# Linear attention without a projection of the values: exponentials of k times the normalised input, then the value weights on the 128x128 result

## What is computed

```
xn = _rmsnorm(x, g1)                                  # over the channels of a token
qkv = jnp.einsum('oc,bchw->bohw', w_qkv, xn)
q, k, v = (qkv[:, 0], qkv[:, 1], qkv[:, 2])
k = jnp.concatenate([mk, k], axis=-1)                 # memory tokens in front
v = jnp.concatenate([mv, v], axis=-1)
q = jax.nn.softmax(q, axis=-2) * attn_scale
k = jax.nn.softmax(k, axis=-1)                        # over the tokens
context = jnp.einsum('bhdn,bhen->bhde', k, v)
out = jnp.einsum('bhde,bhdn->bhen', context, q)
out = jnp.einsum('oc,bchw->bohw', w_out, out) + b_out[None, :, None, None]
return _rmsnorm(out, g2)                               # added to the block's input
```

## Time and profile before

| | us |
|---|---|
| runs | 493.48, 493.88, 495.92 |
| median | 493.88 |
| span of the profiled execution | 491.7 |
| PE busy | 442.3 (90%) |
| DVE busy | 384.4 (78%) |
| ACT busy | 275.3 (56%) |
| POOL busy | 222.1 (45%) |

### The profile page before, as it was taken

One profiled execution on the slowest core, in us unless ns is written; L12 is line 12 of the kernel. 1 busy time (PEld: TensorE's weight loads), 2 busy tenths in 40 slices (PEclk: granted clock), 3 DMA queues, 4 the chain that ended last, 5 costly groups with the idle time before them and its releaser, 6 DMA issues. The chain is left out here.

```text
span 491.7 us, 8244 instructions
## 1 busy us (share of the span) xinstructions
PE 442.3 (90%) x2398; PEld 372.7 (76%) x2398; DVE 384.4 (78%) x754; ACT 275.3 (56%) x828; POOL 222.1 (45%) x187
## 2 busy tenths in 40 slices
PE   2659675999999999999999999999999999998796
PEld 1538464888888888887888888888888888876675
DVE  4461578989798979897988979898989798987531
ACT  2346567574738475657567574848575657552110
POOL 5404345544545372736454455546372736333120
PEclk9977968899999999999999999999999999999799
DMA  7202020203021120303030302012030202021011
GB/s 214 118 0 87 1 87 1 85 3 128 1 86 45 39 91 1 128 0 128 0 128 0 128 0 92 36 47 81 13 117 1 87 0 88 0 87 43 2 43 43
DMA packets 9563, 27.99 MB, mean 57 GB/s; under 512 B 1969, under 2 KB 3009, under 8 KB 9537
## 3 DMA queue, kind: packets, MB, share of 16 engines
q1 hardware_dynamic: 9536, 27.68, 16.0%
HBM read 19.29 MB, written 8.39 MB: 56 GB/s over the span
## 5 line engine op out<-in xcount | busy, mean ns | idle before, releaser
L1126 PE MATMUL ps_conv<-pad_hi,w_lo 128*128 128x512 f32 (+1 forms) x288 | 121.8, 423 | 0.0
L1126 PE MATMUL ps_conv<-pad_hi,w_hi 128*128 128x512 f32 (+1 forms) x288 | 118.7, 412 | 2.9 <-POOL w_lo L496 2.9
L1126 PE MATMUL ps_conv<-pad_lo,w_hi 128*128 128x512 f32 (+1 forms) x288 | 119.4, 414 | 0.0
L549 ACT ACTIVATE qkv<-ps_qkv,scale 128x384 f32<-128x384 f32 x128 | 70.3, 582 | 32.1 <-PE ps_qkv L1046 30.2
L496 POOL TENSOR_TENSOR w_lo<-w_full,w_hi 128x1152 fp32r<-128x1152 f32 x16 | 42.5, 2659 | 92.1 <-ACT w_hi L607 53.7
L464 POOL TENSOR_TENSOR q_exp<-q_exp,q_rsum 128x1024 f32<-128x1024 f32 x16 | 30.6, 1913 | 89.2 <-DVE q_rsum L778 89.2
L1126 PEld LDWEIGHTS ps_conv<-pad_hi,w_lo 128*128 128x128 f32 x288 | 55.6, 193 | 13.5
L1126 PEld LDWEIGHTS ps_conv<-pad_hi,w_hi 128*128 128x128 f32 x288 | 55.7, 193 | 13.0 <-POOL w_lo L496 3.7
L1126 PEld LDWEIGHTS ps_conv<-pad_lo,w_hi 128*128 128x128 f32 x288 | 55.6, 193 | 9.4
L561 ACT ACTIVATE q_exp<-q_exp 128x1024 f32<-128x1024 f32 x16 | 17.0, 1061 | 68.1 <-DVE q_exp L764 68.1
L1044 PE MATMUL ps_qkv<-wqkv_hi,x_hi 128*128 128x384 f32 x128 | 46.1, 360 | 5.2 <-ACT qkv L549 4.7
(11 more groups left out here) (122 smaller groups left out, 980.4 us busy)
## 6 DMA issues: line engine op xcount, KB each, us to landing
xa<-in_x_dram SPq DMA_DIRECT2D x16, 512.0 KB, 4.2
xb<-in_x_dram SPq DMA_DIRECT2D x16, 512.0 KB, 4.9
out_dram<-result SPq DMA_DIRECT2D x16, 512.0 KB, 2.9
expert_raw<-_conv_expert_weight_dram SPq DMA_DIRECT2D x1, 1728.0 KB, 8.8
fc<-in_L_conv_fc_w_dram SPq DMA_DIRECT2D x1, 384.0 KB, 4.3
wqkv_raw<-in_L_conv_w_qkv_dram SPq DMA_DIRECT2D x1, 192.0 KB, 3.4
wout_raw<-in_L_conv_w_out_dram SPq DMA_DIRECT2D x1, 64.0 KB, 2.5
bias_raw<-in_L_conv_b_out_dram SPq DMA_DIRECT2D x1, 64.0 KB, 2.4
```

What stands on the lines that cost most here:

```text
L549: nc.scalar.activation(qkv[:, t, 0:QKV], ps_qkv[t % 2][:, 0:QKV], ACT.Copy, scale=scale1[:, t:t + 1]).then_inc(qkv_done, 1)
L1126: last = mm(into, weight[:, tap, :], pixels[:, top + down:bottom + down, columns_in], start=(n == 0), stop=(n == 3 * TAPS - 1))
```

## The change

The projection computes q and k only (`wqk_hi`, `wqk_lo`; 256 columns instead of 384). The v part is replaced by associativity. While the transposed x is still in `ps_qkv`, ACT copies it to `x_nt` (`x_copy`, twice 128x512, behind each `squares1`), and POOL multiplies it by `scale1` (`x_scale`, 128x1024, behind `filters_low`). `key_contexts` on PE multiplies the exponentials of k by `x_nt`. Its result is divided later: `k_sums` takes the reciprocal of the sums, `k_x_evacuate` (ACT) copies the result out, `key_context_transpose` (PE) transposes it, `x_k_evacuate` (ACT) copies that, and the new `contexts` (PE) multiplies it by the value weights and adds the memory tokens' part. `context_mask` (DVE) keeps the heads' blocks, `mixes` and `mix_evacuate` follow as before, the latter with the reciprocal.

Orders change too. On PE `mixes` moves behind both halves of `x_transpose` and behind `group_variances`; then come two products of the convolution, `routing`, and only then `outputs`. Before it was `mixes`, `x_transpose`, `group_variances`, `outputs`, `routing`. The core of the diff:

```diff
+            def x_scale(b, p):
+                pool.wait_ge(x_nt_done, 2 * (b + 1))
+                pool.wait_ge(scale1_done, b + 1)
+                nc.gpsimd.tensor_tensor(x_nt[:, :, 0:C], x_nt[:, :, 0:C],
+                                        scale1[:, :].unsqueeze(2).to_broadcast((128, NT, C)),
+                                        ALU.mult).then_inc(x_scaled_done, 1)
...
                 do(filters_low, t, p, 4)
+                do(x_scale, t, p, 2)
                 do(q_normalise, t, p, 2)
...
+            def x_copy(b, p, h):
+                if past(b, 1):
+                    act.wait_ge(k_x_ps, b)
+                act.wait_ge(ssq1_sum_done, 2 * b + h + 1)
+                nc.scalar.activation(x_nt[:, NT // 2 * h:NT // 2 * (h + 1), 0:C],
+                                     ps_qkv[h][:, :].rearrange("p (t c) -> p t c", c=C), ACT.Copy).then_inc(x_nt_done, 1)
...
-                nc.scalar.activation(qkv[:, t, 0:QKV], ps_qkv[t % 2][:, 0:QKV], ACT.Copy, scale=scale1[:, t:t + 1]).then_inc(qkv_done, 1)
+                nc.scalar.activation(qk[:, t, :], ps_qkv[t % 2][:, 0:QK], ACT.Copy, scale=scale1[:, t:t + 1]).then_inc(qkv_done, 1)
...
+                do(k_x_evacuate, t, p, 2)
                 do(q_evacuate, t, p, 2, 0)
-                do(context_evacuate, t, p, 2)
+                do(x_k_evacuate, t, p, 2)
                 do(q_evacuate, t, p, 2, 1)
                 do(image_high, t, p, 3)
                 do(squares1, t, p, 1, 0)
+                do(x_copy, t, p, 1, 0)
                 do(squares1, t, p, 1, 1)
+                do(x_copy, t, p, 1, 1)
...
+                do(context_mask, t, p, 2)
                 do(gn2_centre, t, p, 3)
                 do(mix_evacuate, t, p, 2)
                 turn(variances, t, p, 0)
...
-                do(context_sums, t, p, 1)
+                do(k_sums, t, p, 1)
                 do(gn2_aggregate, t, p, 2)
-                do(context_scale, t, p, 1)
...
-                mm(o, x1_hi[:, tile(t)], wqkv_hi[:, :], start=True, stop=False)
+                mm(o, x1_hi[:, tile(t)], wqk_hi[:, :], start=True, stop=False)
...
+            def key_contexts(b, p):
                 pe.wait_ge(memk_exp_done, b + 1)
                 pe.wait_ge(k_exp_done, b + 1)
+                pe.wait_ge(x_scaled_done, b + 1)
+                mm(ps_att[:, 0:CEXT], memk_exp[:, :], mem_ones[:, :], start=True, stop=False)
                 for t in range(NT):
+                    last = mm(ps_att[:, 0:CEXT], k_exp[:, t, :], x_nt[:, t, :], start=False, stop=(t == NT - 1))
+                last.then_inc(k_x_ps, 1)
+
+            def contexts(b, p):
+                pe.wait_ge(x_k_done, b + 1)
+                mm(ps_att[:, 0:HID], memv_t[:, :], memk_exp[:, :], start=True, stop=False)
+                mm(ps_att[:, 0:HID], wqkv_t[:, QK:QKV], x_k[:, :], start=False, stop=True).then_inc(context_ps, 1)
...
                 conv(4)
-                do(contexts, t, p, 2)
+                do(key_contexts, t, p, 2)
                 conv(2)
                 do(q_transpose, t, p, 2, 0)
                 do(q_transpose, t, p, 2, 1)
-                do(context_transpose, t, p, 2)
+                do(key_context_transpose, t, p, 2)
                 turn(group_means, t, p, 0)
                 conv(2)
-                do(mixes, t, p, 2)
+                do(contexts, t, p, 2)
                 do(x_transpose, t, p, 1, 0)
                 turn(group_variances, t, p, 0)
...
                 do(x_transpose, t, p, 1, 1)
+                do(mixes, t, p, 2)
+                conv(2)
+                do(routing, t, p, 3)
                 do(outputs, t, p, 2)
-                do(routing, t, p, 3)
-                conv(4)
+                conv(2)
                 do(project, t, p, 1, 0)
```

More of the change, by code:

```diff
@@ L56, in attention_condconv_kernel @@
     QKV = 3 * HID
-    VEXT = HID + 2
+    QK = 2 * HID
+    CEXT = C + 2
     GN_EPS, NORM_MIN = 1e-5, 1e-12
@@ L134, in attention_condconv_kernel @@
         k_rsum = sb("k_rsum", [128, 1])
+        k_x = sb("k_x", [128, C])
+        x_k = sb("x_k", [128, HID])
         context = sb("context", [128, HID])
-        context_t = sb("context_t", [128, HID])
         q_t = [sb(f"q_t{p}", [128, N]) for p in range(2)]
@@ L234, in attention_condconv_kernel @@
         q_norm_done = sem("q_norm_done")
+        x_nt_done = sem("x_nt_done")
+        x_scaled_done = sem("x_scaled_done")
+        k_x_ps = sem("k_x_ps")
+        k_rsum_done = sem("k_rsum_done")
+        k_x_done = sem("k_x_done")
+        x_k_ps = sem("x_k_ps")
+        x_k_done = sem("x_k_done")
         context_ps = sem("context_ps")
-        k_rsum_done = sem("k_rsum_done")
         context_done = sem("context_done")
-        context_t_ps = sem("context_t_ps")
-        context_t_done = sem("context_t_done")
         mix_ps = sem("mix_ps")
@@ L518, in _ @@
             act.wait_ge(setup_dve, 1)
-            nc.scalar.activation(wqkv_hi[:, :], wqkv_t[:, :], ACT.Copy).then_inc(setup_act, 1)
+            nc.scalar.activation(wqk_hi[:, :], wqkv_t[:, 0:QK], ACT.Copy).then_inc(setup_act, 1)
             def squares1(b, p, h):
@@ L561, in q_exponent, with k_x_evacuate, x_k_evacuate @@
                 nc.scalar.activation(q_exp[:, :, :], q_exp[:, :, :], ACT.Exp).then_inc(q_exp_done, 1)
-            def context_evacuate(b, p):
-                act.wait_ge(context_t_ps, b + 1)
+            def k_x_evacuate(b, p):
+                act.wait_ge(k_x_ps, b + 1)
+                act.wait_ge(k_rsum_done, b + 1)
                 if past(b, 1):
-                    act.wait_ge(mix_ps, b)
-                nc.scalar.activation(context_t[:, :], ps_att[:, 0:HID], ACT.Copy).then_inc(context_t_done, 1)
+                    act.wait_ge(x_k_ps, b)
+                nc.scalar.activation(k_x[:, :], ps_att[:, 0:C], ACT.Copy).then_inc(k_x_done, 1)
+            def x_k_evacuate(b, p):
+                act.wait_ge(x_k_ps, b + 1)
+                if past(b, 1):
+                    act.wait_ge(context_ps, b)
+                nc.scalar.activation(x_k[:, :], ps_att[:, 0:HID], ACT.Copy).then_inc(x_k_done, 1)
             def q_evacuate(b, p, h):
@@ L1039, in project @@
                 if t < 2:
-                    pe.wait_ge(ssq1_sum_done, 2 * b + t + 1)
+                    pe.wait_ge(x_nt_done, 2 * b + t + 1)
                 if t >= 2:
                     pe.wait_ge(qkv_done, NT * b + t - 1)
-                o = ps_qkv[t % 2][:, 0:QKV]
-                mm(o, x1_hi[:, tile(t)], wqkv_hi[:, :], start=True, stop=False)
-                mm(o, x1_hi[:, tile(t)], wqkv_lo[:, :], start=False, stop=False)
-                mm(o, x1_lo[:, tile(t)], wqkv_hi[:, :], start=False, stop=True).then_inc(qkv_ps, 1)
+                o = ps_qkv[t % 2][:, 0:QK]
+                mm(o, x1_hi[:, tile(t)], wqk_hi[:, :], start=True, stop=False)
+                mm(o, x1_hi[:, tile(t)], wqk_lo[:, :], start=False, stop=False)
+                mm(o, x1_lo[:, tile(t)], wqk_hi[:, :], start=False, stop=True).then_inc(qkv_ps, 1)
             def k_part_transpose(b, p):
```

62 lines of the change are left out of this document (31 added, 31 removed).

## The result

The changed kernel took 585.95 us (median of 4 runs, 581.99 to 587.2) against 493.68 for the kernel before in the same comparison (493.19 to 495.92). The ratio is 1.184, with a 95% interval of 1.179 to 1.190. The forecast was 572 with a range of 533 to 594: the sign and the places of the loss were right, the size was 14 us short. The profiled execution has a span of 585.3 us.

A forecast was written before the change was run, and what follows sets the result against it. PE bounds the kernel before by its own work. Steps of 30.5 us and four long cases add 64.3 us, the ends 5, the clock 9: span 570.0, plus 2.2 makes 572 us, range 533 to 594.

The forecast's parts named there:

- R to K: Start of routing product to start of exponentials' product: late outputs delay squares, first copies and DVE's chain; +1.79 us a step.
- The projection: On PE, 24 products of 256 instead of 384 columns: 1.40 us less a step, swallowed by waits.
- x_scale: Scaling of x on POOL behind w_lo holds q_subtract on DVE for 1.85 us: +1.55 us a step.
- Rival 1: DVE's two operations slip in before x_scale, or lose only a fifth of its length: 550 us, chance 0.28.
- K to R: Exponentials' product to next routing product: uncovered chain from gvar takes 2.34 us; 9.09 against 8.06, +1.03 us a step.
- The long case: In the chain gvar to routing product, pad_lo begins before rstd: 3.29 us instead of 2.34; 0.92 added in four steps.
- The clock: PE's clock falls behind the waits before the routing product: seven steps at 1.3 us each, 9 us.
- rival 2: PE's clock falls in nearly every step, at 1.95 us, on top of the forecast: 592 us, chance 0.12.
- The ends: Outside the 14 steps: two more hand-overs in one step, waits before the first and behind the last routing product; +5 us.
- 3: Rival: PE's clock never falls and DVE's operations slip in before x_scale; 541 us, chance 0.14.
- 5: Rival: the change does not do what it says; chance 0.06 for faster or unchanged together.
- 4: Rival, between gvar and routing product: PE stays the bound, 12 us gained, 482 us; chance 0.06 for faster or unchanged together.

The follow-up runs named there:

- two runs: Kernel after with the scaling of x on POOL moved right behind rms1, 568.59 us; kernel after with that scaling cut to one channel, 569.37 us.
- the kernel with the filler: Kernel after plus 17 products of 128x256 on PE just before each routing product, their result overwritten: 569.58 us, ratio 1.153.
- the last kernel: Kernel after with outputs ahead of routing, variances first on DVE, scaling on ACT, and convolution products respread: 495.8 us, ratio 1.002.

## Why the prediction was right, and where its sizes were off

**What bounds the kernel, and the main cause: right.** PE's new order makes the routing chain end without cover and the outputs late. Alone in the kernel before it costs 73 us; the outputs alone moved back in the kernel after give 53.

**R to K: right.** Forecast and measured, as distances from R: outputs' squares until 4.5, first copies at 4.53; third project tile waits until 4.95, measured 5.11; L839 at 4.55, measured 4.72; residual at 7.8, measured 7.87; end of w_lo 15.4, measured 15.31; k_shift 15.6, measured 15.52. K was to come at 19.86 + 1.1 = 20.96 with the scaling and came at 20.82. These are the rows of the undisturbed step; with the falls of the clock the mean is 22.05.

**The projection: right in size, right that it is swallowed.** Records of 256 columns follow each other at 0.12 us (0.117 forecast).

**x_scale: the mechanism right, the price a little high.** Of the two operations of DVE it was q_subtract that was held, k_diag slipped in before, as taken. It costs 1.2 us a step (17 us in all by two runs) and not 1.55, in part since the hold was 1.71 and not 1.85. Rival 1, that both slip in, is out: the subtraction takes 2.92 in every step between 90 and 450 us.

**K to R: the step that failed.** 9.09 and 0.45 for DVE's lateness were forecast, 10.17 came. gvar starts at K + 7.16, as it should (6.75 + 0.45), but the chain from there to the routing product takes 3.01 and not 2.34. "The long case comes in four of the 14 steps" was carried over from the kernel before. In the kernel after rstd has 1.67 us as the median of the steps, 1.44 the least. What made the case rare can be read in other steps of the kernel before, DVE and POOL:

```profile
149.40 0.16 DVE L716 TENSOR_SCALAR gvar<-ps_stat 128x2 f32<-128x2 f32 x1 [0.16 <-PE ps_stat L1024]
149.79 1.28 DVE L856 SCALAR_TENSOR_TENSOR pad_lo<-x,nmean,pad_hi 128x1024 fp32r<-128x1024 f32 x1 [0.23 <-ACT pad_hi L589]
...
361.03 1.31 DVE L856 SCALAR_TENSOR_TENSOR pad_lo<-x,nmean,pad_hi 128x1024 fp32r<-128x1024 f32 x1
...
361.07 0.70 POOL L433 TENSOR_TENSOR rstd<-gvar,minus_half 128x2 f32<-128x2 f32 x1 [1.42 <-DVE gvar L716]
```

Either pad_lo still had to wait for pad_hi of ACT, or it was ahead of rstd by only 0.04 us and rstd got through; with 0.20 ahead rstd was held. After the change gvar comes later against ACT, pad_hi has been there for over a microsecond (in the step shown it ended at 431.87, and pad_lo started at 433.12), and pad_lo is ahead of rstd by 0.15 to 0.39 in all 14 steps, mostly by 0.16. I had counted how often the case came and not asked what decides it. The run with variances first has rstd at 0.70 or less in all steps, but it doesn't price the hold, since pooled_n is held there instead.

The 2.34 itself was no undisturbed chain, as the prediction has it. pad_lo held pooled_n in that step, which took 0.51 instead of 0.22 and ended 0.08 behind pad_lo:

```profile
230.93 0.22 POOL L479 TENSOR_TENSOR pooled_n<-pooled_c,rstd 128x16 f32<-128x16 f32 x1
...
361.91 0.51 POOL L479 TENSOR_TENSOR pooled_n<-pooled_c,rstd 128x16 f32<-128x16 f32 x1
```

So pad_lo delays the chain in both kinds of steps, through rstd or through pooled_n. No run takes it out of the way; what the chain would be without it is not shown. In the sum the 3.01 makes an undisturbed step 31.0 and not 30.5 + 0.26, some 4 us.

**The clock: mis-sized.** Seven falls at 1.3 us, 9 us in all, were forecast; 11 of the 14 steps have a clock below 1.00, and their mean above the undisturbed 31.04 is 1.6 us (452.2 - 14 x 31.04 = 17.6; 17.6 / 11). That takes every step for as long as the three undisturbed ones. Step against step, the kernel with the filler gives 14.5 us for ten falls, 1.46 each; the first step has a fall in both, as in the kernel before. The medians of the two kernels differ by 16. So it was the number of falls that was too small. That is the mixture of forecast and rival 2: the falls came nearly every step as rival 2 said, but at less than 1.95 on average (two reached 2.1).

**The ends.** 585.3 - 452.2 = 133.1 us lie outside of the 14 steps, against 125.3 before: 7.8 more, where +5 and the clock's share of 0.6 had been put.

So the missing 15 us of the span are 9 from the clock (17.6 for 8.4), 4 from rstd held by pad_lo with what K to R had besides, and 2 from the ends. With the filler as the measure it is 6 from the clock (14.5 for 8.4), 7 from the steps at full clock (437.7 for 430.7) and 2 from the ends.

**Rivals 3 to 5.** The clock fell, so 3 is out. The projection's rows have 256 columns and PE's rows stand in the new order, so 5 is out. For 4, that PE stays the bound, the decisive point was whether `mixes` is through before K + 5.5: it started at K + 6.47. The run with PE's outputs ahead, variances first and the scaling on ACT shows what brings PE back as the bound: three more edits. With the convolution respread it comes to no measurable difference and not to 482, since PE's busy time fell by only 0.1 us a step.

**What isn't settled.** Which of the steps lose the clock: with the wait at 1.92 to 2.00 us (variances first) it fell in some and not in others of equal wait, and in the kernel after it held at 1.00 behind three waits of 2.82 (373.90, 405.07, 436.06) and fell behind others of 2.82. How much of K to R is the hold by pad_lo: no run has the chain without it. And where the rest of PE's saving goes, 0.46 us a step by its records and 0.1 by its busy time; the last kernel was not taken apart.

## What to carry to other kernels

Before a product is moved behind a wait, count it as cover and look at who is queued behind its result: 1.95 us of outputs covered the routing chain here, the squares, the copies and DVE's chain hung on them, and the order of three calls cost 73 us. A delay that appears in some steps of a trace is decided by the order of two queues; ask whether the change makes it the rule instead of carrying its frequency over. Work put on POOL should be checked against what DVE does at that time with two inputs from SBUF; ACT, with slack before a wait, took the same work here without a loss that shows (2.44 us for the eight copies, with 1.85 of its wait still left).
